# Cross attention's context columns turned for two heads at once, and two products for the delta layer's running sums

## The reference

```python
def _L1_xattn_ref(draft_hidden, context_hidden, Wq, Wk, Wv, Wo, q_norm_w, k_norm_w, ...):
    q = _rms_norm((draft_hidden @ Wq.T).reshape(bsz, draft_len, H, HD), q_norm_w).transpose(0, 2, 1, 3)
    kv_in = jnp.concatenate([context_hidden, draft_hidden], axis=1)
    k = _rms_norm((kv_in @ Wk.T).reshape(bsz, total_len, KVH, HD), k_norm_w).transpose(0, 2, 1, 3)
    v = (kv_in @ Wv.T).reshape(bsz, total_len, KVH, HD).transpose(0, 2, 1, 3)
    q, k = _rope(q, draft_position_ids), _rope(k, full_position_ids)
    k, v = jnp.repeat(k, N_REP, axis=1), jnp.repeat(v, N_REP, axis=1)
    probs = jax.nn.softmax(jnp.einsum('bhqd,bhkd->bhqk', q, k) * SCALE, axis=-1)
    attn = jnp.einsum('bhqk,bhkd->bhqd', probs, v)
    return attn.transpose(0, 2, 1, 3).reshape(bsz, draft_len, H * HD) @ Wo.T
```

```python
alpha = jax.nn.sigmoid(x @ Wa)      # one gate per token and head, 16 heads
beta = jax.nn.sigmoid(x @ Wb)
def step(state, inp):
    qt, kt, vt, at, bt = inp
    state = state * at[:, :, None, None]
    ...
```

## Time and profile before

| | us |
|---|---|
| median of 3 runs | 4089.55 |
| the profiled execution's own time | 4080.05 |
| its span, first to last instruction | 4078.2 |
| cross attention's stages | from about 2917 to about 3820 of the span |
| the delta layer's part ahead of its stages | 1114 to 1152 of the span |

### The profile page before, as it was taken

One profiled execution on the slowest core, in us unless ns is written; L12 is line 12 of the kernel. 1 busy time (PEld: TensorE's weight loads), 2 busy tenths in 40 slices (PEclk: granted clock), 3 DMA queues, 4 the chain that ended last, 5 costly groups with the idle time before them and its releaser, 6 DMA issues. The chain is left out here.

```text
span 4078.2 us, 59075 instructions
## 1 busy us (share of the span) xinstructions
PE 3568.7 (88%) x17488; PEld 2739.0 (67%) x17488; DVE 2668.5 (65%) x7918; ACT 1676.4 (41%) x4266; POOL 1407.4 (35%) x2115
## 2 busy tenths in 40 slices
PE   7999997499688999999999999998499999999665
PEld 5767675355366888888888888886366666666453
DVE  5666665622257888888888888873676676676521
ACT  3444443233234554555545455541244444444221
POOL 0000000078515555555555555553111111111055
PEclk9999998599778999999999999999699999999765
DMA  2000004245501111111111111110100000000456
GB/s 77 0 0 0 0 0 112 77 80 83 108 14 28 36 35 30 37 27 37 27 38 27 39 28 37 28 21 11 59 1 0 0 0 0 0 0 0 118 119 138
DMA packets 220952, 150.06 MB, mean 37 GB/s; under 512 B 116976, under 2 KB 208656, under 8 KB 220208
## 3 DMA queue, kind: packets, MB, share of 16 engines
q1 hardware_dynamic: 193664, 111.55, 10.8%
q0 software_dynamic: 22848, 31.69, 4.7%
q10 hardware_dynamic: 4224, 4.19, 0.3%
HBM read 105.71 MB, written 41.61 MB: 36 GB/s over the span
## 5 line engine op out<-in xcount | busy, mean ns | idle before, releaser
L1998 DVE SCALAR_TENSOR_TENSOR dl_y<-ps,dl_taps,dl_y 128x255 f32<-128x255 f32 (+2 forms) x1536 | 653.2, 475 | 128.5 <-ACT dl_y L1894 124.3
L1729 PE MATMUL ps<-xnT,dl_wkqv 128*128 128x256 f32 x2048 | 543.3, 391 | 29.8 <-DVE dl_lp L2041 21.6
L1729 PEld LDWEIGHTS ps<-xnT,dl_wkqv 128*128 128x128 f32 x2048 | 368.8, 194 | 81.2 <-issue 35.4
L519 PE MATMUL ps<-at_shared,at_v 128*128 128x256 f32 (+2 forms) x1280 | 320.9, 382 | 56.4 <-DVE at_shared L689 29.4
L1652 POOL TENSOR_TENSOR dl_rn<-dl_n,mhalf 128x4 f32<-128x4 f32 x128 | 173.1, 1352 | 550.4 <-DVE dl_n L2014 550.4
L519 PEld LDWEIGHTS ps<-at_shared,at_v 128*128 128x128 f32 (+1 forms) x1280 | 206.5, 188 | 164.6 <-issue 111.2
L431 POOL TENSOR_TENSOR at_rs<-at_ss,mhalf 64x1 f32<-64x1 f32 x32 | 55.4, 1731 | 742.3 <-DVE at_ss L623 742.3
L1894 ACT ACTIVATE dl_y<-ps,dl_taps 128x256 f32<-128x256 f32 x512 | 260.1, 559 | 103.1 <-PE ps L1729 103.1
L454 PE MATMUL ps<-at_wq,at_xb 128*128 (+1 forms) x512 | 244.8, 612 | 39.6 <-POOL at_xb L425 33.8
L1670 POOL TENSOR_TENSOR dl_inv_u<-dl_inv_u,dl_inv_tmp 64x30 f32<-64x30 f32 (+14 forms) x480 | 260.7, 543 | 37.6
L490 PE MATMUL ps<-at_kT,at_qT 128*128 128x320 f32 (+2 forms) x1024 | 257.7, 385 | 1.4 <-ACT at_kT L745 1.4
(11 more groups left out here) (362 smaller groups left out, 7935.6 us busy)
## 6 DMA issues: line engine op xcount, KB each, us to landing
dl_grow<-decay_rows SPq DMA_DIRECT2D x128, 128.0 KB, 3.1
sp_wgu<-in_w1gu SPq DMA_DIRECT2D x12, 768.0 KB, 5.8
dl_wkqv<-in_w1kqv SPq DMA_DIRECT2D x16, 512.0 KB, 4.6
delta_diag<-dl_lp SPq DMA_DIRECT2D x512, 8.0 KB
dl_diag<-delta_diag_tt SPq DMA_DIRECT2D x512, 8.0 KB, 1.7
moe_wgu<-in_w0gu SPq DMA_DIRECT2D x16, 448.0 KB, 12.0
sp_wd<-in_w1d SPq DMA_DIRECT2D x12, 384.0 KB, 6.8
dl_wo<-in_w1o SPq DMA_DIRECT2D x16, 256.0 KB, 3.7
```

Source lines behind the costliest of these rows:

```text
L519: last = nc.tensor.matmul(slot(h, (r % 2) * 4 + 3)[:, c0:S], v[h][0:w, j, :], pT[h][0:w, r % 2, j, c0:S], start=j == 0, stop=j == KT - 1)
L1729: last = nc.tensor.matmul(bank(h, m // 2, (m % 2) * S, (m % 2 + 1) * S), wkqv[h][:, c, m * P:(m + 1) * P], k.xnT[:, c, u.seq * S:(u.seq + ...
L1998: last = nc.vector.scalar_tensor_tensor(y[h][:, m, back:S], bank(h, m // 2, (m % 2) * S, (m % 2 + 1) * S - back), taps[h][:, m, KC - 1 - b ...
```

## The change

The context tile is made 128 rows high by holding the 64 context tokens twice: GpSimd copies them to `xb` twice, and from there the projection, rotation, squares, `ss`, `rs`, `v` and the turned keys have 128 rows where they had 64. The rotation tables of the context (`CrossRope`: `cc`, `sc`, `cpos` and their temporaries) have 128 rows too, and the position input holds its 64 rows twice. ACT keeps the turned keys as context, own, context (one copy more, of 64 columns). An even head scores against own and context, an odd head against context and own. Since the probabilities of an even head and the following odd head now lie next to each other, the 128 columns in the middle of the two are the context columns of both. One transpose per token tile turns them (`context_pair`), with the even head's in rows 0 to 63 and the odd head's in rows 64 to 127. DVE copies them once for each pair. The even head's mix reads rows 0 to 63 of the values' context tile and the odd head's rows 64 to 127. ACT's copy of the other columns no longer waits for the context's transposes (`probs_turned` comes before them, `pair_turned` behind), and the even head's mix waits for DVE's copy only ahead of its last product.

In the delta layer the 24 products become two: the triangle over all 256 columns of `loga`, and the square of ones over the 8 x 16 columns of each sequence's first tile, added to the second. PE's wait for `made` moves from ahead of the gates to behind the running sums.

The diff, without the rotation tables' shapes and the lines that only widen a 64-row operand to 128:

```diff
@@ -333,11 +333,11 @@
         def sb(name, shape, dt=F32):
             return k.sb(f"at{k.attn_calls}_{name}", shape, dt, st)
 
-        xb = [sb(f"xb{h}", [P, DC, NK]) for h in range(2)]
+        xb = [sb(f"xb{h}", [P, DC, KT * P]) for h in range(2)]
         t1 = [sb(f"t1{h}", [P, KT, G + 1, HD]) for h in range(2)]
         t2 = [sb(f"t2{h}", [P, KT, G + 1, HD]) for h in range(2)]
         qT = [sb(f"qT{h}", [P, G, S]) for h in range(2)]
-        kT = [sb(f"kT{h}", [P, NK]) for h in range(2)]
+        kT = [sb(f"kT{h}", [P, CTX + NK if cross else NK]) for h in range(2)]
         v = [sb(f"v{h}", [P, KT, HD]) for h in range(2)]
         mx = [sb(f"mx{h}", [P, 4]) for h in range(2)]
         nb = [sb(f"nb{h}", [P, 4]) for h in range(2)]
...
@@ -377,6 +377,22 @@
 
         def seen(t):
             return NK if cross else (t + 1) * P
+
+        def prob(h, r, t):
+
+            return probs[h][:, t * 2 + r % 2, 0:NK] if cross else probs[h][:, (r % 2) * TB + t, 0:seen(t)]
+
+        def own(h, r, t):
+
+            return prob(h, r, t)[:, (r % 2) * CTX:(r % 2) * CTX + S]
+
+        def context_pair(h, t):
+
+            return probs[h][:, :, :].rearrange("p m s -> p (m s)")[:, t * 2 * NK + S:t * 2 * NK + S + 2 * CTX]
+
+        def keys(h, r, t):
+            c0 = CTX * (1 - r % 2) if cross else 0
+            return kT[h][:, c0:c0 + seen(t)]
 
...
@@ -422,13 +438,15 @@
                     wait_before(pool, s.projected[h], u * 3)
                     xc = nc.gpsimd.tensor_copy(xb[h][:, :, 0:S], k.xnT[:, :, ds(turn(u) * (2 * S) + h * S, S)])
                     if cross:
-                        xc = nc.gpsimd.tensor_copy(xb[h][:, :, S:NK], ctx.ctxT[:, :, ds(turn(u) * (2 * CTX) + h * CTX, CTX)])
+                        for c0 in (S, S + CTX):
+                            xc = nc.gpsimd.tensor_copy(xb[h][:, :, c0:c0 + CTX],
+                                                       ctx.ctxT[:, :, ds(turn(u) * (2 * CTX) + h * CTX, CTX)])
                     xc.then_inc(s.xb_ready[h], 1)
 
                 def invert_rms(h, u):
 
                     pool.wait_ge(s.sq_done[h], u + 1)
-                    nc.gpsimd.tensor_tensor(rs[h][0:CTX, TB, G:G + 1], ss[h][0:CTX, TB, G:G + 1], k.mhalf[0:CTX, 0:1], ALU.pow)
+                    nc.gpsimd.tensor_tensor(rs[h][:, TB, G:G + 1], ss[h][:, TB, G:G + 1], k.mhalf[:, 0:1], ALU.pow)
                     nc.gpsimd.tensor_tensor(rs[h][:, 0:TB, :], ss[h][:, 0:TB, :],
                                             k.mhalf[:, 0:TB * (G + 1)].rearrange("p (t g) -> p t g", t=TB), ALU.pow)\
                         .then_inc(s.rms_ready[h], 1)
...
@@ -473,7 +491,7 @@
                         for t in range(TB):
                             nc.tensor.transpose(slot(h, hh)[:, t * P:(t + 1) * P], t1[h][:, t, hh, :], k.ident[:, :])
                     for t in range(KT):
-                        r = krows[t]
+                        r = P
                         last = nc.tensor.transpose(k.ps[h][:, 2, t * P:t * P + r], t1[h][0:r, t, G, :],
                                                    k.ident[0:r, 0:r])
...
                             last.then_inc(s.scored[h], 1)
                     if not cross:
                         last.then_inc(s.scored[h], 1)
 
                 def turn_probs(h, u, r):
-                    for t in range(TB):
-                        if cross:
-                            pe.wait_ge(s.probs_ready[h], u * (G * TB) + (r * TB + t + 1))
-                        elif t == 0:
-                            pe.wait_ge(s.probs_ready[h], u * G + (r + 1))
-                        for j in range(TB):
-                            if cross or j <= t:
-                                last = nc.tensor.transpose(slot(h, (r % 2) * 4 + pieces[j])[:, t * P:(t + 1) * P],
-                                                           probs[h][:, (r % 2) * TB + t, j * P:(j + 1) * P], k.ident[:, :])
                     if cross:
                         for t in range(TB):
-                            last = nc.tensor.transpose(slot(h, (r % 2) * 4 + pieces[TB])[0:CTX, t * P:(t + 1) * P],
-                                                       probs[h][:, (r % 2) * TB + t, S:NK], k.ident[:, :])
-                    last.then_inc(s.probs_turned[h], 1)
+                            pe.wait_ge(s.probs_ready[h], u * (G * TB) + (r * TB + t + 1))
+                            for j in range(TB):
+                                last = nc.tensor.transpose(slot(h, (r % 2) * 4 + j)[:, t * P:(t + 1) * P],
+                                                           own(h, r, t)[:, j * P:(j + 1) * P], k.ident[:, :])
+                        last.then_inc(s.probs_turned[h], 1)
+                        if r % 2:
+                            for t in range(TB):
+                                last = nc.tensor.transpose(slot(h, 6)[:, t * P:(t + 1) * P], context_pair(h, t), k.ident[:, :])
+                            last.then_inc(s.pair_turned[h], 1)
+                    else:
+                        pe.wait_ge(s.probs_ready[h], u * G + (r + 1))
+                        for t in range(TB):
+                            for j in range(t + 1):
+                                last = nc.tensor.transpose(slot(h, (r % 2) * 4 + pieces[j])[:, t * P:(t + 1) * P],
+                                                           prob(h, r, t)[:, j * P:(j + 1) * P], k.ident[:, :])
+                        last.then_inc(s.probs_turned[h], 1)
 
                 def mix(h, u, r):
+                    o = slot(h, (r % 2) * 4 + 3)
                     pe.wait_ge(s.probs_kept_a[h], u * G + (r + 1))
-                    pe.wait_ge(s.probs_kept_d[h], u * G + (r + 1))
-                    for j in range(KT):
-                        w = krows[j]
+                    if not cross:
+                        pe.wait_ge(s.probs_kept_d[h], u * G + (r + 1))
+                    elif r % 2:
+                        pe.wait_ge(s.probs_kept_d[h], u * 2 + (r // 2 + 1))
+                    for j in range(TB):
                         c0 = 0 if cross else j * P
-                        last = nc.tensor.matmul(slot(h, (r % 2) * 4 + 3)[:, c0:S], v[h][0:w, j, :],
-                                                pT[h][0:w, r % 2, j, c0:S], start=j == 0, stop=j == KT - 1)
+                        last = nc.tensor.matmul(o[:, c0:S], v[h][:, j, :], pT[h][:, r % 2, j, c0:S],
+                                                start=j == 0, stop=not cross and j == TB - 1)
+                    if cross:
+                        if r % 2 == 0:
+                            pe.wait_ge(s.probs_kept_d[h], u * 2 + (r // 2 + 1))
+                        n0 = (r % 2) * CTX
+                        last = nc.tensor.matmul(o, v[h][n0:n0 + CTX, TB, :], pT[h][n0:n0 + CTX, 0, TB, :], start=False, stop=True)
                     last.then_inc(s.mixed[h], 1)
 
                 def give(h, u):
...
@@ -682,14 +712,17 @@
                         norm_head(h, u, r + 1)
 
                 def keep_probs(h, u, r):
-
                     dve.wait_ge(s.probs_turned[h], u * G + (r + 1))
-                    piece = slot(h, (r % 2) * 4 + 2)
+                    nc.vector.tensor_copy(pT[h][:, r % 2, 1, P:S], slot(h, (r % 2) * 4 + 2)[:, P:S]).then_inc(s.probs_kept_d[h], 1)
+
+                def keep_pieces(h, u, r):
+
                     if cross:
-                        last = nc.vector.tensor_copy(pT[h][0:CTX, r % 2, TB, :], piece[0:CTX, :])
+                        dve.wait_ge(s.pair_turned[h], u * 2 + (r // 2 + 1))
+                        nc.vector.tensor_copy(pT[h][:, 0, TB, :], slot(h, 6)).then_inc(s.probs_kept_d[h], 1)
                     else:
-                        last = nc.vector.tensor_copy(pT[h][:, r % 2, 1, P:S], piece[:, P:S])
-                    last.then_inc(s.probs_kept_d[h], 1)
+                        keep_probs(h, u, r)
+                        keep_probs(h, u, r + 1)
 
                 def add_out(h, u):
                     dve.wait_ge(s.out_ready[h], u + 1)
...
@@ -734,15 +765,19 @@
 
                         nc.scalar.activation(sqs[h][:, 0:TB, 0:G, :], q_ps(h), ACT.Square)
                         nc.scalar.activation(sqs[h][:, 0:TB, G, :], kv_ps(h, 0), ACT.Square)
-                        nc.scalar.activation(sqs[h][0:CTX, TB, G, :], ckv_ps(h, 0), ACT.Square)\
+                        nc.scalar.activation(sqs[h][:, TB, G, :], ckv_ps(h, 0), ACT.Square)\
                             .then_inc(s.projected_sq[h], 1)
-                        nc.scalar.copy(v[h][0:CTX, TB, :], ckv_ps(h, 1))
+                        nc.scalar.copy(v[h][:, TB, :], ckv_ps(h, 1))
                     nc.scalar.copy(v[h][:, 0:TB, :], kv_ps(h, 1)).then_inc(s.v_kept[h], 1)
 
                 def keep_qk(h, u):
                     act.wait_ge(s.qk_turned[h], u + 1)
                     nc.scalar.copy(qT[h][:, :, :], k.ps[h][:, 0:2, :].rearrange("p a (b s) -> p (a b) s", b=2))
-                    nc.scalar.copy(kT[h][:, :], k.ps[h][:, 2, 0:NK]).then_inc(s.qk_kept[h], 1)
```

(43 more changed lines are left out.)

21 lines of the change are left out of this document (10 added, 11 removed).

## The result

The changed kernel is slower: 4130.32 us, median of three runs (4129.96 to 4135.87), against 4089.55. The ratio is 1.0105, with a 95% interval of 1.0082 to 1.0128. The forecast was 4068, its range 4057 to 4080.

What follows compares the result with a forecast made beforehand. It took a loop of waits through all engines to bound cross attention's stages, and a plain chain the delta layer's opening. Savings of 10.9 (delta) and 10.4 us (cross attention), 21.3 off 4089.55, gave 4068; range 4057 to 4080.

Steps and rivals of the forecast that it cites:

- heads 2 and 3: Cross attention: most of the first mix's 0.94 us wait goes, gaining nothing, since the second mix still starts with ACT's copy.
- My sign of being wrong: Cross attention: a stage period not shorter than 27.90 us would mean a branch held for early was late.
- PE's branch: Cross attention: last mix, then output product, parallel to the loop; taken as some 0.2 to 0.25 us early.
- The loop: Cross attention: one chain of waits through all engines sets the stage; 0.32 us less each, period 27.5 to 27.6.
- GpSimd's third copy: Cross attention: the added 0.29 us copy beside DVE's scaling costs the loop 0.10 us a stage, bounds 0 and 0.29.
- rival 1: Cross attention: the added GpSimd copy stops DVE's scaling for its whole 0.29 us; kernel 4074.5 us, chance 0.13.
- the lock: SBUF port pair of DVE and GpSimd: first comer keeps it; the added copy could hold DVE's scaling its whole time, not 0.10.
- GpSimd's power: Cross attention's loop: going from 64 x 1 to 128 x 1 changes nothing, about 1.73 us; bounds 0.23 more, 0.64 less.
- Rival 4: Cross attention: GpSimd's power takes time by rows, +1.73 us in each of 31 stages; slower, 4122 us, chance 0.05.
- The delta layer: Its opening: 2.1 us from the moved wait, 8.8 from sums taking 1.65 instead of 10.43; 10.9 saved, bounds 8.5 to 12.5.
- all rivals but one: Five rivals across both parts: 4074.5 us (chance 0.13), 4078.6 (0.08), 4057.7 (0.10), 4122 (0.05) and 4079 (0.04).

Runs made afterwards that it cites:

- wait_ahead: Changed kernel, but the even head's mix waits for DVE's copy of the context pair ahead of its first product; ratio 1.0005 to the kernel before.
- fill2: Changed kernel with two added products (0.86 us, result unused) between the mixes of heads 2 and 3; ratio 0.9921 to the kernel before.
- keep_early: Changed kernel with ACT's copy of head 3's turned probabilities ahead of the squares and value copies; ratio 0.9946 to the kernel before.
- delta_alone: Kernel before with only the delta layer part of the change; ratio 0.9954 to the kernel before.
- fill_late: Changed kernel with two added products behind the output product, ahead of the turning of the keys; ratio 1.0066 to the kernel before.

## Why the prediction was wrong

- **The step that failed** is that on heads 2 and 3: "Most of that goes, and brings nothing". The wait of 0.94 did go, the last mix did still start with ACT's copy, and I booked the moved idle at zero. It cost the clock: the 31 periods took 65 us more, where 10 less were forecast. `wait_ahead` (the wait put back, 28 of 31 periods at the full clock) and `fill2` (the idle filled, all of them) show that the merged idle is what cost it. All durations of my sum were taken at 1.00 granted, and no rival let that change in cross attention. My sign of being wrong, a period that is not shorter, came up, but not for the reason that stands there: PE's branch was late only through the lower clock. `fill2` shows that this was the only error of size there.
- **The loop** was right: 27.5 to 27.6 us forecast, 27.58 in `fill2` and 27.57 in `keep_early`, which keep the clock and have all of the change. The scores still waited for ACT, and ACT's copy was released by L520, as said.
- **GpSimd's third copy** stretched the three scalings from 0.76 to 0.80 us, so by 0.04 and not by my 0.10, let alone rival 1's 0.29 or the whole copy's time by the lock.
- **GpSimd's power** over 128 x 1 took 1.73 us, as over 64 x 1. Rival 4 was wrong; the sign came out its way by another mechanism.
- **The delta layer**: 1.64 us for the sums (1.65 forecast) and 12.3 us in the opening (10.9). The rest is clock, and luck: PE began the gates while it still had 1.00 granted, and the 64 passes took 12.38 us, not 13.83. In `delta_alone` they took 13.83, and the opening was 10.8 shorter, as forecast. The gain arrived: stages of cross attention began 13.8 us earlier. Single profiles scatter in that start, by 14 us among the nine with the delta part, but their mean is 12.9 earlier than that of the three without it.
- The range ended at 4080 because all rivals but one were sums of small costs. The stretch where PE already had its largest idle piece was in the rows, and I did not ask what moving it up to the next one does.

## What to carry to other kernels

A wait that is moved behind part of the work it held need not remove idle time: here it collected it, 0.94 and 0.23 us into 1.40. Where PE runs at the full clock with several small idle pieces close together, read the granted clock by window after every change of waits: here the lost clock cost some 2.4 us a stage, where all that the change saved was 0.3. Where the idle can't be removed, try to move it between dense passes (`keep_early`), or fill it with passes whose result nobody reads (`fill2`).

## What the runs showed of the hardware

- The clock depends on where idle lies. With 1.40 us before the last mix it was lost in every stage of the changed kernel and in every second one of `fill_late`, with the same piece before the mix of head 2 in the old kernel in about a third of the stages, and with 1.49 us between dense passes in none. The Trainium skill (TensorE: Matmul & The Clock Gate, "A second HAM failure mode: psum-queue depth-cycling") says of another kernel, in bf16, that frequent short idle between groups of matmuls made the clock swing between its two levels. The trace agrees: 1.00 and 0.50 in turn, 0.90 in the mean. What exactly the chip weighs is not shown by these runs.
- A GpSimd power that started beside a DVE addition with two SBUF inputs took 3.28 us, and 2.11 without, for the same 128 x 11. It ended 1.98 us after the addition, as if it had waited for it. The 1.73 us of the small power before the change is probably mostly this wait too: the addition beside it ends at 3393.99 and the power 0.42 later. That was not tried apart. The Trainium skill (SBUF — State Buffer, "Who interferes with whom") states that such a DVE instruction contends with a GpSimd instruction that reads SBUF; the trace agrees.
- Where a product of 64 rows followed one of 128 rows in the mixes, its weight load came after 0.33 us in which the profile shows no wait, with the change (L550 at 3411.37 above) and without it.

The addition and the weight load of the kernel before, for the last two points:

```profile
3392.52 1.47 DVE L610 TENSOR_TENSOR at_t<-at_t 128x1280 f32<-128x1280 f32 x1
...
3392.65 0.29 PEld L519 LDWEIGHTS ps<-at_shared,at_v 64*128 64x128 f32 x2 [0.33 <-issue]
```
